# Two expert tiles of a mixture-of-experts stage prepared inside the stage before, and their table built in the first tile

## What is computed

```python
logits = x @ router_w + router_b
topk_scores, topk_idx = top_k(logits, 2)
gates = softmax(topk_scores)
# for each expert e, with c[e] the token's gate for it (0 if it wasn't chosen)
h = relu(x @ W1[e] + b1[e]);  out += (h @ W2[e] + b2[e]) * c[e]
```

## Time and profile before

| | |
|---|---|
| median of 3 runs | 1032.37 us (1029.37 to 1032.58) |
| the profiled execution | 1034.7 us, span 1032.9 us |
| instructions | 17927 |
| busy: TensorE, its weight loads | 896.7 us (87%), 766.0 us (74%) |
| busy: VectorE, ScalarE, POOL | 797.3 us (77%), 606.9 us (59%), 558.7 us (54%) |
| mean granted clock of TensorE | 0.943 |
| DMA | 139.11 MB, mean 135 GB/s |

### The profile page before, as it was taken

The page is one execution under the profiler, slowest core; times in us unless marked ns, Lnnn a source line. Parts: engine busy times, 40 slices in busy tenths (PEclk is TensorE's granted clock), DMA queues, the critical chain, the costliest instruction groups (busy, mean ns, idle before and its releaser), DMA issues.

```text
span 1032.9 us, 17927 instructions
## 1 busy us (share of the span) xinstructions
PE 896.7 (87%) x5742; PEld 766.0 (74%) x5742; DVE 797.3 (77%) x2026; ACT 606.9 (59%) x1166; POOL 558.7 (54%) x461
## 2 busy tenths in 40 slices
PE   4789888888745079999999999999999999999993
PEld 3456555565534069989999999998998998998993
DVE  1699999999995367787787787787778778779761
ACT  2688889898862045555564555565556556555541
POOL 1114565656575354565565576567457557556434
PEclk8899999999975579999999999999999999999997
DMA  8334454533124564465554565457547546556423
GB/s 270 123 104 142 124 154 123 154 116 100 47 47 55 94 212 126 129 148 181 150 143 127 153 197 139 117 166 202 122 127 220 132 128 148 196 138 140 127 26 41
DMA packets 71682, 139.11 MB, mean 135 GB/s; under 512 B 10925, under 2 KB 62766, under 8 KB 67658
## 3 DMA queue, kind: packets, MB, share of 16 engines
q0 software_dynamic: 31136, 98.34, 36.4%
q1 hardware_dynamic: 40490, 40.08, 13.9%
HBM read 110.52 MB, written 27.86 MB: 134 GB/s over the span
## 4 chain that ended last, share of the span: by engine, by line
PE 58%; DVE 4%; issue 1%; POOL 1%; ACT 0%; DMA 0%; DVEq 0%; ACTq 0%; POOLq 0%
PE hp L1387 28%; PE acc L1399 28%; PE xt L1374 2%; DVE wlo L1423 2%; DVE xlo L1427 1%; DVE ysum L1463 1%; DVE hhi L1478 1%; POOL out_rows L1314 1%; DVE hlo L1480 0%; DMA h<-token_rows,tile_tid 0%; ACT hid L1352 0%; POOL h L147 0%; ACT yout L1342 0%; ACT xhi L1325 0%; ACTq L1232 0%
## 5 line engine op out<-in xcount | busy, mean ns | idle before, releaser
L1352 ACT ACTIVATE hid<-hp,b 128x512 f32<-128x512 f32 (+1 forms) x248 | 158.9, 641 | 293.0 <-PE hp L1387 291.0
L1399 PE MATMUL acc<-whi,hhi 128*128 128x256 f32 x880 | 246.3, 280 | 0.0
L1399 PE MATMUL acc<-wlo,hhi 128*128 128x256 f32 x880 | 245.6, 279 | 0.0
L1399 PE MATMUL acc<-whi,hlo 128*128 128x256 f32 x880 | 245.4, 279 | 0.0
L1478 DVE CAST hhi<-hid 128x512 fp32r<-128x512 f32 (+1 forms) x248 | 105.0, 423 | 140.1 <-ACT hid L1352 139.1
L1314 POOL DMA_INDIRECT out_rows<-yout,dest x110 | 182.1, 1656 | 57.1 <-issue 31.7
L1387 PE MATMUL hp<-xhi,whi 128*128 128x512 f32 (+1 forms) x496 | 186.1, 375 | 10.9 <-DVE xlo L1427 8.3
L371 POOL DMA_INDIRECT expert_lists<-tid,slots x96 | 135.8, 1414 | 95.9 <-DVE slots L935 71.3
L1387 PE MATMUL hp<-xlo,whi 128*128 128x512 f32 (+1 forms) x496 | 183.2, 369 | 0.0
L1387 PE MATMUL hp<-xhi,wlo 128*128 128x512 f32 (+1 forms) x496 | 182.9, 369 | 0.0
L1399 PEld LDWEIGHTS acc<-wlo,hhi 128*128 128x128 f32 x880 | 165.8, 188 | 7.9
(11 more groups left out here) (185 smaller groups left out, 1434.4 us busy)
## 6 DMA issues: line engine op xcount, KB each, us to landing
xin<-in_x SPq DMA_DIRECT2D x32, 512.0 KB
xin<-in_x SPq DMA_DIRECT2D x32, 256.0 KB
token_rows<-xs SPq DMA_DIRECT2D x16, 388.5 KB, 4.8
out_rows<-h SPq DMA_DIRECT2D x16, 384.0 KB, 3.0
h<-token_rows,tile_tid POOLq DMA_INDIRECT x110, 5.4
out_rows<-yout,dest POOLq DMA_INDIRECT x110, 4.0
expert_lists<-tid,slots POOLq DMA_INDIRECT x96
out_rows<-zrow SPq DMA_DIRECT2D x1, 512.0 KB
```

The lines of the kernel that those rows point to most:

```text
L1352: act.activation(hid[:, c % 2, 0:j.r * P], hp[c % 2][:, 0:j.r * P], ACT.Relu, bias=b1[:, j.s, c:c + 1]).then_inc(hid_done, 1)
L1399: last = pe.matmul(acc_of(j, r), h_[:, c % 4, r * P:(r + 1) * P], w_[:, j.s, at:at + C], start=c == 0 and n == 0 and r % 2 == 0, stop=c == ...
```

## The change

It does five things.

1. **Two tiles are chosen early.** Once pair 10 has been placed (11 pairs known), six small VectorE instructions find the expert with the most tokens so far, which then has at least 1024, and write the indices of tiles 0 and 1: the first 1024 places of its list.
2. **They are fetched in the last rounds by POOL.** In the round of pair 15 (`first_lists`, `first_rows`) and in the first drain round (`second_tile`), each with waits for what it needs. `h_read` waits until the residuals whose memory the fetch overwrites have been read.
3. **Tile 0 is split and transposed in the drain rounds,** in buffers that lie over the input frames and the set-up constants: ScalarE 3 and 5 pieces of `whi` and both of `xhi`, VectorE 3, 3 and 2 pieces of `wlo` and both of `xlo`, TensorE eight transposes in the first drain round.
4. **The table of the other tiles is made in tile 0,** its steps dealt out behind `w_low` of chunks 0 to 6, the copy of tile 2's indices last. It leaves out the 1024 places that tiles 0 and 1 take (`gone`, `region`). `mark` of tile 0 comes in chunk 1.
5. **The last pair's scatter** moves from the token stage into POOL's list of the expert stage, and the waits for all lists and rows stand in front of tile 2's fetch (`all_listed`). SP's wait for the rows, and `all_rows`, go.

POOL, token stage:

```diff
+            def first_lists():
+                pool.wait_ge(tables.idx_ready, AHEAD)
+                h_read(WROW)
+                fetch.weights(t0)
+                for s in range(2):
+                    pool.wait_ge(listed[s], 96 * len(range(s, KNOWN, 2)))
+                fetch.tokens(t0)
+                fetch.tokens(t1)
+
+            def first_rows():
+                for s in range(XS):
+                    pool.wait_ge(rows_stored[s], 16 * len(range(s, KNOWN, XS)))
+                pool.wait_ge(tables.tid_in[0], 16)
+                h_read(2 * WROW + R * ROW)
+                fetch.rows(t0, KNOWN * PAIR_TOK)
+
+            def second_tile():
+                h_read(2 * WROW)
+                fetch.weights(t1)
+                pool.wait_ge(tables.tid_in[1], 16)
+                h_read(2 * (WROW + R * ROW))
+                fetch.rows(t1, KNOWN * PAIR_TOK)
+
             def body(p0, p1, p2, p3, p4):
                 if p1:
                     seeds(p1)
-                if p4:
-                    scatter(p4)
+                if p0.q == PAIRS - 1:
+                    first_lists()
+                if p4:
+                    fetch.scatter(p4)
+                if p0.q == PAIRS - 1:
+                    first_rows()
 
             def drain(p1, p2, p3, p4):
                 if p1:
                     seeds(p1)
-                if p4:
-                    scatter(p4)
+                if p4.q < PAIRS - 1:
+                    fetch.scatter(p4)
+                if p1:
+                    second_tile()
 
             rounds(body, drain)
-
-            fetch, t0 = Fetch(pool, tables, ew, rows, lists), Tile(0, 0)
-            pool.wait_ge(tables.idx_ready, 1)
-            fetch.weights(t0)
-            for s in range(2):
-                pool.wait_ge(listed[s], 96 * (PAIRS // 2))
-            fetch.tokens(t0)
-            pool.wait_ge(all_rows, 1)
-            pool.wait_ge(tables.tid_in[0], 16)
-            fetch.rows(t0)
```

ScalarE, TensorE and VectorE in the drain:

```diff
                     log_sigmoid(p1)
+                    first_weights(range(0, 3))
                     log_divisor(p1)
+                if p2 and not p1:
+                    first_weights(range(3, FC))
+                    first_rows()
                 if p2:
                     root_2(p2)
...
                 if p2:
                     project(p2)
+                if p1:
+                    first_rows()
...
                     sigmoid_divisor(p1)
+                if p2 and not p1:
+                    first_weights(range(0, 3))
+                if p3 and not p2:
+                    first_weights(range(6, FC))
+                    first_rows()
                 if p3:
                     lg_in(p3)
...
                     selected(p3)
+                if p2 and not p1:
+                    first_weights(range(3, 6))
                 if p2:
                     residual(p2)
```

Expert stage, POOL and VectorE:

```diff
             def first():
-                pool.wait_ge(idx_ready, 2)
-                fetch.tokens(T0.nxt())
-                fetch.weights(T0.nxt())
+                fetch.scatter(Pair(PAIRS - 1))
                 gather_b2(T0)
-                gather_x(T0.nxt())
...
                 a, n, p = j.after(), j.nxt(), j.prev()
+                if j.first():
+                    all_listed()
                 if a.exists():
                     pool.wait_ge(idx_ready, a.at(1, 1))
...
                         w_low(n, c)
-                    if c == 1 and a.exists():
+                    if j.first():
+                        if c == 0:
+                            whole_tiles()
+                        if c == 1:
+                            mark(j)
+                            remainders()
+                        if c == 2:
+                            shares()
+                        if c == 3:
+                            first_groups()
+                        if c == 4:
+                            experts_of_tiles()
+                        if c == 5:
+                            groups_of_tiles()
+                        if c == 6:
+                            rows_of_table()
+                            indices(dve, tables, a)
+                    elif c == 1 and a.exists():
```

More of the change, by code:

```diff
@@ L99 @@
 XS = 3
+N_PLACE = 9
+KNOWN = 11
+AHEAD = 2
+assert -(-KNOWN * PAIR_TOK * 2 // E) >= AHEAD * TS
 class Tables:
@@ L131, in __init__, with scatter @@
     def __init__(self, pool, tables, ew, rows, lists):
-        self.pool, self.tables, self.ew, self.rows_of = pool, tables, ew, rows
+        self.pool, self.tables, self.ew, self.rows_of, self.lists = pool, tables, ew, rows, lists
         self.groups = {n: lists.rearrange("(g r) a -> g (r a)", r=n) for n in (R, RH)}
+    def scatter(self, q):
+        t = self.tables
+        self.pool.wait_ge(t.placing, q.at(N_PLACE, N_PLACE))
+        for c in range(6):
+            self.pool.indirect_dma_start(self.lists, bass.IndirectOffsetOnAxis(t.slots[:, q.q, c:c + 1], 0),
+                                         t.tokens[:, q.q, c % 3:c % 3 + 1], None).then_inc(t.listed[q.s], 16)
     def weights(self, j):
@@ L228, in tokens_to_experts @@
         m1, m2, i1, i2, dm, ed, ed1 = (sb(n, [P, 3]) for n in ("m1", "m2", "i1", "i2", "dm", "ed", "ed1"))
[L229 to L244, removed]
+        slots = tables.slots
+        counts, top, is_top = sb("counts", [P, E]), sb("top", [P, 1]), sb("is_top", [P, E])
+        numbers, fullest = tables.fewer, tables.fullest
         conv_ps, wo_ps, kr_ps = ps("conv_ps", 2), ps("wo_ps", 2), [ps("kr_ps0"), ps("kr_ps1")]
@@ L948, in body @@
                     weighted_sum(p2)
+                if p4 and p4.q == KNOWN - 1:
+                    known_counts()
                 statistic_1(p0, 1)
+                if p4 and p4.q == KNOWN - 1:
+                    most()
                 statistic_1(p0, 2)
+                if p4 and p4.q == KNOWN - 1:
+                    has_most()
                 mean_1(p0, 0)
@@ L962, in body @@
                     second_places(p4)
+                if p4 and p4.q == KNOWN - 1:
+                    first_indices()
                 if p3:
@@ L1159, in _ @@
-            step(dve.tensor_scalar(table[:, :, 0], ecl[:, :], float(P), part[:, R:R + 1], ALU.mult, ALU.add))
-            indices(dve, tables, Tile(0, 0))
-            indices(dve, tables, Tile(0, 1))
 class Tile:
@@ L1204, in rows_in_slot, with tiles @@
         return self.q * (16 * per_q) + 16 * ((self.i // 2) * R + more)
-def tiles(eng, first, body):
-    first()
+def tiles(eng, body):
     for i in range(4):
@@ L1362, in body @@
                         x_high(n, c - 4)
-            tiles(act, first, body)
+            tiles(act, body)
             gated(LAST)
@@ L1412, in body @@
                         transposes(j.nxt())
-            tiles(pe, lambda: transposes(T0), body)
+            tiles(pe, body)
             down(LAST, FC - 2)
@@ L1467, in first, with over_tiles, over_experts @@
                 bias(T0)
-                for k in range(FC):
-                    w_low(T0, k)
-                    if k in (3, 4):
-                        x_low(T0, k - 3)
-                mark(T0)
+            def over_tiles(a, n=NC):
+                return a.unsqueeze(1).to_broadcast([P, n, E])
+            def over_experts(a, n=NC):
+                return a.unsqueeze(2).to_broadcast([P, n, E])
+            big, half, rest = slice(AHEAD, NB), slice(NB, NC), slice(AHEAD, NC)
+            steps = [0]
@@ L1503, in body @@
                         mark(n)
-            tiles(dve, first, body)
+            first()
+            tiles(dve, body)
             sums(LAST)
```

321 lines of the change are left out of this document (207 added, 114 removed).

## The result

The changed kernel takes **1021.38 us** (median of 5 runs, 1019.1 to 1024.23) against 1032.37 us (5 runs, 1029.37 to 1033.86) of the kernel before on the same chip: ratio 0.9902, 95% interval 0.9883 to 0.9921. It is faster, as forecast, but by 11 us and not by 20: the forecast was 1012.3 us, and the median lies just outside the range of 1004 to 1021. Measured a second time, the same pair gave 1023.46 us and a ratio of 0.9913 (0.9895 to 0.9931).

A forecast was written before the change was run, and what follows sets the result against it. The bound was TensorE, busy except for a 34.85 us seam between token stage and expert tiles. 33.35 - 6.1 - 4.5 - 2.7 = 20.05 us off the median 1032.37 gave 1012.3 us, range 1004 to 1021.

The forecast's parts named there:

- Term 1: Seam before tile 0: of 34.85 us only a handover of 1.5 us (1.4 to 6) stays; gain 33.35 us.
- Terms 2 and 3: Late token stage: six VectorE instructions and POOL's new wait and row fetches end it 6.1 us later (3.5 to 12).
- term 2: Round of pair 10: six small VectorE instructions, all on the path, cost 0.6 us, at most 1.3.
- Rival A: Before pair 11's scatter: POOL waits longer for pair 10's scatters, 5.6 us more on the path, 1018 us; chance 0.14.
- Term 4: Drain rounds: splits and transposes of tile 0 hide in existing waits and cost nothing; transposes run near 307.
- Term 5: Tile 0: the table on VectorE delays x_low of tile 1, so TensorE loses 4.5 us (0 to 7).
- Term 6: Tile 1: tile 2's late indices delay its weights; loss 2.4 us, 2.7 with the clock (0 to 7).
- B: Row fetches and table: better hidden, terms 3, 5 and 6 fall to 4, 2 and 0; 1005.6 us; chance 0.18.
- C: From the first up matmul: TensorE's clock stays low through tiles 0 and 1, 13 us slower, 1045; chance 0.03.
- D: Behind the seam: a resource such as POOL makes the tiles wait anyway, nothing gained, 1031; chance 0.03.

The follow-up runs named there:

- all_four: Changed kernel with both orders mended, no GpSimd drain, and the wait for the token stage's last stores taken out of SyncE's stage end; 1022.76 us, ratio 0.9882 to the kernel before.

## Why the prediction was right or wrong, point by point

- **What bounds the kernel: right.** The 34.85 us of the seam went, and what came in their place stood in the sum with the right name, but for the end of the kernel and a thin drift.
- **Term 1, the handover: right.** 1.0 us for 1.5. A late store of SyncE, for which its upper bound of 6 stood, came in a profile of a later kernel (4.9).
- **Terms 2 and 3, the new wait of POOL: right in mechanism, 1.4 us too small, and this is one of the steps that failed.** The last scatter of pair 10 is issued at 276.21 for 275.67, 0.5 us later: term 2 had 0.6. The four row fetches took 5.1 us, as forecast. The overrun of 0.4 us before them was wrong: the step that failed is that the last scatter "lands by about 281". POOL was released at 284.9, the two token fetches followed, and the scatter of pair 11 started at 288.62, 4.8 us later than in the earlier trace rows, so that the overrun was 4.2 us. Two things that the sum did not have took most of this back: the six scatters took 9.3 us and not 10.9, and from the scan to the last slots it was 0.7 us less than before. Rival A had 10.5 us from the end of the last issue to the release; it was 7.4.
- **Term 4, splits and transposes of tile 0 hidden: right.** ScalarE's and VectorE's pieces caused no new wait; the path from the scan to the slots was no longer than before (303.33 to 341.79, 38.5 us; 295.11 to 334.26, 39.2). The transposes of tile 0 came at 306.4, forecast 307.
- **Term 5, the table in tile 0: exact.** First up of tile 1 at +27.8 us, forecast 27.8, 0.1 us behind the end of `xlo`, and VectorE had no wait from the first `hhi` on.
- **Term 6, tile 2's list: the step that failed most, 3.5 us.** The order of events was right (list at 369.77, weights issued at 372.73, ScalarE's wait, TensorE's idle time before the fourth up). Two sizes were wrong.
  - *"that hid, ready at 38.5".* It was ready at 383.24 - 342.83 = 40.4. The list was complete when the sum had it (27.1 us after the first up), but POOL issued the tokens 1.15 us later, where it had been 0.2 us before (344.21 to 344.41), and the tokens' issue took 1.6 us for 1.3, so the weights left at 29.9 and not at 28.5. They landed after 9.27 us for 8.8. So the fourth up came 383.28 - 370.63 = 12.65 us after the first, where it had been 8.28 before (400.67 - 392.39): a loss of 4.4 us for 2.4. In the repeated execution it was 4.6.
  - *The clock, 0.3 us.* After the 5.3 us of idle time the first up group took 373.33 - 370.63 = 2.70 us for 1.38, and with the down behind it 1.4 us were lost. This slow start ate into the wait for the weights, as I had written: TensorE's idle time there was 2.77 us and not some 4.2, since `hid` came when the weights let it. But after these 2.77 us the clock fell a second time, behind the last wait, where nothing could hide it, and the next two groups took 4.62 us for 2.77, 1.85 us more. In the repeated execution the second fall did not come, and the whole term was 15.8 - 10.9 = 4.9 us and not 6.2.

  The estimate of 6.8 us made from the Trainium skill, DMA: Bandwidth & Descriptors, "Anatomy of one DMA", is further off: this transfer took 9.27 us, and in the token stage the weights of tile 0 took 12.4 and those of tile 1 took 14.1.
- **A term that was missing: the end.** I took the time behind the last tile as given, a term of 0 without a reason. It grew by 3.3 us, all of it in GpSimd's drain. Nothing in the trace of before could have told the size, but its length of 5.3 us was there to be asked about.
- **A drift: open.** From tile 2's transposes to the last store the changed kernel takes 1.7 us more than before (before, three profiles: 622.0 to 622.8 us; with the change, ten profiles without all_four: 624.4 to 624.6 us in eight, 625.6 in the two others). It is spread thinly over the 29 tiles, about 0.06 us each, and no run here tells where it comes from.
- **The rivals.** B did not come: neither the row fetches nor the table got cheaper. C did not come in its own form, since tile 0 was at the full clock by 347, about 4 us in and so no later than before, but its cause, the low clock, struck again after the new waits. D's price (1031) was paid only where tile 1's fetch was put back.

Of the 9.5 us that were missing, 7.8 have a place that a run or a row shows: 1.4 in POOL's wait for the scatters, 3.5 in tile 1 (2.0 for the late weights, 1.5 for the second fall of the clock), 3.3 in the drain, less 0.5 of a shorter handover; the drift is the rest. What makes the drain longer, and where the drift comes from, stays open.

## What to carry to other kernels

When work is moved past a seam to be hidden, price each new wait of TensorE twice: the wait, and the groups behind it at half the clock. What is slow ahead of another wait can vanish in it (1.4 us here); what is slow behind the last one is lost (1.85 us in one execution, nothing in the repeated one). Put the smallest instruction that another engine waits for ahead of a row of DMA issues: 0.2 us of seeds in front of four fetches was worth 5.7 us. And compare what lies behind the last row of the two kernels before giving a gain to the whole: an end that nobody touched took back 3.3 of 13.8 us.

## What the runs showed of the hardware that I had not expected

- GpSimd's drain at the end of the kernel took 2.7 us in one kernel and 6.1 us in another with the same number of DMA issues. In every profile the end was as long as in the others of its kernel: 5.3 us in both of before, 8.5 to 8.7 in the eight of kernels with the change and the drain.
- From the end of the last issue of a pair's six scatters to the release of the waiting queue it took 6.0 to 7.4 us in the eleven profiles of kernels with the change, and 7.4 us both in the changed kernel, with 2.1 MB of weights beside them, and in the one without.
- In tile 1, at the same place of seven profiles, idle times of 1.9, 2.0 and 2.4 us were followed by work at a granted clock of 1.00, those of 2.6, 2.8, 3.0 and 3.0 us by work at 0.50. In the changed kernel the clock was back at 1.00 some 3 us after work resumed behind the 5.3 us and some 4 us behind the 2.8; behind the 4.55 us of the repeated execution it took some 5.
